# A quantized matrix turned by VectorE in 32x32 blocks, with the block exchange in its store

## The reference

```
xn  = layernorm(x)
s   = causal_attention(xn)            # 32 query heads of 16, one shared key and value head, projected by wo
h   = linear8bit(xn, W1, b1)          # 512 -> 2048
g   = silu(linear8bit(h, W2, b2))     # 2048 -> 512
out = x + s * g

linear8bit(a, W, b): columns of a whose largest |value| is over 3 are outliers;
    y = quant_rows(a without outliers) @ quant_rows(W).T + (outliers of a) @ W.T + b
quant_rows(a): scale = max|row| / 127;  round(a / scale) * scale
```

## Time and profile before

| | us |
|---|---|
| median of three timed runs | 802.89 |
| lowest and highest | 801.82, 803.98 |
| span of the profiled execution | 800.2 |
| PE busy in it | 766.0 |
| DVE busy | 639.8 |
| ACT busy | 404.4 |
| POOL busy | 255.5 |
| attention block, some | 96 to 407 |
| W1 products, some | 409 to 603 |

### The profile page before, as it was taken

One profiled execution on the slowest core, in us unless ns is written; L12 is line 12 of the kernel. 1 busy time (PEld: TensorE's weight loads), 2 busy tenths in 40 slices (PEclk: granted clock), 3 DMA queues, 4 the chain that ended last, 5 costly groups with the idle time before them and its releaser, 6 DMA issues. The chain is left out here.

```text
span 800.2 us, 12098 instructions
## 1 busy us (share of the span) xinstructions
PE 766.0 (96%) x4253; PEld 579.9 (72%) x4253; DVE 639.8 (80%) x1099; ACT 404.4 (51%) x686; POOL 255.5 (32%) x335
## 2 busy tenths in 40 slices
PE   5999899999999999999999999999997999999995
PEld 4878565656676676775578888888886888888884
DVE  7988989999999999995537476666658998599957
ACT  4354166767777666777634544544553333132212
POOL 7213135555555555554521110110100000036504
PEclk9999689999999999999999999999999999999998
DMA  7431303333322223334454443222013778436982
GB/s 265 147 106 53 82 15 87 83 81 85 99 81 83 82 82 85 95 110 123 163 198 150 153 158 138 93 73 79 27 48 101 246 223 259 162 106 223 342 276 105
DMA packets 58348, 103.37 MB, mean 129 GB/s; under 512 B 8480, under 2 KB 16688, under 8 KB 56752
## 3 DMA queue, kind: packets, MB, share of 16 engines
q1 hardware_dynamic: 58288, 102.60, 40.2%
HBM read 52.76 MB, written 36.70 MB: 112 GB/s over the span
## 5 line engine op out<-in xcount | busy, mean ns | idle before, releaser
L931 DVE TENSOR_REDUCE rowmax<-ps 128x2 f32<-128x512 f32 (+3 forms) x384 | 210.6, 590 | 20.3 <-PE ps L1008 18.7
L852 ACT ACTIVATE probs<-ps 128x512 f32<-128x512 f32 (+1 forms) x352 | 175.3, 557 | 71.8 <-PE ps L1021 70.1
L1008 PE MATMUL ps<-km,stack 128*128 128x256 f32 (+3 forms) x512 | 150.3, 348 | 2.6 <-PEq L193 1.9
L1021 PE MATMUL ps<-stack,ks 128*128 128x512 f32 (+1 forms) x352 | 132.8, 387 | 2.6 <-ACT probs L852 2.6
L1008 PEld LDWEIGHTS ps<-km,stack 128*128 128x128 f32 (+1 forms) x512 | 95.1, 199 | 43.1 <-DVE rowmax L931 23.9
L834 POOL TENSOR_SCALAR_AFFINE_SELECT probs<-probs 128x512 f32<-128x512 f32 x128 | 81.0, 641 | 78.0 <-ACT probs L852 76.6
L1823 PE MATMUL ps<-big_h 128*128 128x512 f32 x256 | 100.5, 393 | 2.3 <-issue 2.0
L1825 PE MATMUL ps<-big_h,big_l 128*128 128x512 f32 x256 | 100.1, 391 | 0.0
L1824 PE MATMUL ps<-big_l,big_h 128*128 128x512 f32 x256 | 100.1, 391 | 0.0
L1034 PE MATMUL ps<-probs,vones 128*32 128x512 f32 (+3 forms) x1024 | 82.2, 439 | 0.2 <-POOL probs L834 0.2
L1021 PEld LDWEIGHTS ps<-stack,ks 128*128 128x128 f32 x352 | 67.4, 192 | 11.6 <-ACT probs L852 6.3
(11 more groups left out here) (227 smaller groups left out, 1388.8 us busy)
## 6 DMA issues: line engine op xcount, KB each, us to landing
stack<-big_h SPq DMA_DIRECT2D x128, 64.0 KB, 2.0
h_scratch<-hs SPq DMA_DIRECT2D x7, 1024.0 KB, 4.5
hload<-h_scratch SPq DMA_DIRECT2D x14, 512.0 KB, 5.0
xn_scratch<-xa SPq DMA_DIRECT2D x4, 1024.0 KB, 4.4
stack<-big_l SPq DMA_DIRECT2D x64, 64.0 KB, 2.0
xi<-xn_scratch SPq DMA_DIRECT2D x16, 256.0 KB, 2.7
xe_scratch<-xm SPq DMA_DIRECT2D x16, 256.0 KB, 2.3
w2n<-in_L_ffn_W_dram SPq DMA_DIRECT2D x4, 1024.0 KB, 6.4
```

Source lines behind the costliest of these rows:

```text
L852: nc.scalar.activation(probs[p][:, o:o + nh * w], ps[:, STB[n % NST], 0:nh * w], ACT.Exp).then_inc(s_exp, 1)
L931: nc.vector.tensor_reduce(dst, src, AX_X, ALU.max).then_inc(s_red, 1)
L1008: last = nc.tensor.matmul(dst, stack[u % 3][rows, hp, P * qt:P * (qt + 1)], km[rows, u // KT, p0:p0 + npar, keys], start=True, stop=True)
L1021: ins = nc.tensor.matmul(ps[:, STB[n % NST], 0:nh * w].rearrange("p (h q) -> p h q", h=nh), ks[:, u // KT, p, P * kt:P * (kt + 1)], stack[ ...
```

## The change

DVE transposes in place of PE. Its transpose turns each 32x32 block of a 128x512 tile on its own and leaves the blocks where they are. For a whole 128x128 transpose the blocks must change places too, row block a with column block b within each group of 128 columns. That exchange is put into the store of the quantized tile: four DMAs (`HB`), one for each 32 rows of the tile, write each run of 32 floats to its exchanged place in `xe_scratch`. Loads of that scratch stay as they were; all counts of `s_xes` become four times as large. In the tail, one transpose by DVE stands at the step where PE had four, ahead of the low part of the tile before. In the FFN block `turn_x` of tiles 12 to 15 stands on DVE between `scale_w1(1)` and the low parts; PE's four groups go, ACT's `high_x` waits for `s_tt`, and the counts of `s_aux` are four lower.

```
@@ second block: setup @@
+        HB, SQ = 4, 32
@@ second block: SP @@
                     if u >= 0:
                         sp.wait_ge(s_xe, u + 1)
-                        sp.dma_start(xe_d[P * u:P * (u + 1), :], xm[:, :]).then_inc(s_xes, 16)
+                        for b in range(HB):
+                            sp.dma_start(xe_d[P * u:P * (u + 1), :]
+                                         .rearrange("(a j) (k b i) -> b j k a i", a=HB, k=KT, b=HB)[b],
+                                         xm[SQ * b:SQ * (b + 1), :].rearrange("j (k a i) -> j k a i", k=KT, a=HB)
+                                         ).then_inc(s_xes, 16)
                     i = tail_tile(g, -5)
                     if i >= 0:
-                        sp.wait_ge(s_xes, 16 * (i + 1))
+                        sp.wait_ge(s_xes, 16 * HB * (i + 1))
...
@@ second block: POOL @@
                         if u:
-                            pool.wait_ge(s_xes, 16 * u)
+                            pool.wait_ge(s_xes, 16 * HB * u)
@@ second block: DVE, after quantize_x, ahead of tail_tile(g, 2) @@
+                    i = tail_tile(g)
+                    if i >= 0:
+                        dve.wait_ge(s_tr[i % 2], 16 * (i // 2 + 1))
+                        if i < NMAX:
+                            dve.wait_ge(s_red, CH * U)
+                        else:
+                            dve.wait_ge(s_xlo, i - NMAX + 1)
+                        nc.vector.transpose(ps[:, MAXB[i % NMAX], :], tail_rows[:, i % 2, :]).then_inc(s_tt, 1)
@@ second block: PE @@
-                    i = tail_tile(g)
-                    if i >= 0:
-                        pe.wait_ge(s_tr[i % 2], 16 * (i // 2 + 1))
-                        if i < NMAX:
-                            pe.wait_ge(s_red, CH * U)
-                        else:
-                            pe.wait_ge(s_xlo, i - NMAX + 1)
-                        for k in range(KT):
-                            last = nc.tensor.transpose(ps[:, MAXB[i % NMAX], P * k:P * (k + 1)],
-                                                       tail_rows[:, i % 2, P * k:P * (k + 1)], ident[:, :])
-                        last.then_inc(s_tt, 1)
@@ third block: ACT @@
                 def high_w1(f):
                     n = aux_at[("w1", f)]
-                    act.wait_ge(s_aux, n + 1)
+                    act.wait_ge(s_aux, n + 1 - (NT - EARLY))
...
                 def high_x(i):
                     n = aux_at[("x", i)]
-                    act.wait_ge(s_aux, n + 1)
+                    act.wait_ge(s_tt, i + 1)
...
@@ third block: DVE @@
+                def turn_x(i):
+                    n = aux_at[("x", i)]
+                    dve.wait_ge(s_xel[i - EARLY], 16)
+                    nc.vector.transpose(ps[:, 4 + n % 4, :], xe[i - EARLY]).then_inc(s_tt, 1)
...
                 scale_w1(1)
                 for f in range(FT):
                     if f == 0:
+                        for i in range(EARLY, NT):
+                            turn_x(i)
                         for i in range(EARLY, NT):
                             low_x(i)
                         low_w1(1)
@@ third block: PE @@
-                def transpose_x(i):
-                    dst = aux_bank(("x", i))
-                    pe.wait_ge(s_xel[i - EARLY], 16)
-                    for k in range(KT):
-                        last = nc.tensor.transpose(dst[:, P * k:P * (k + 1)], xe[i - EARLY][:, P * k:P * (k + 1)],
-                                                   ident[:, :])
-                    last.then_inc(s_aux, 1)
...
                     for c in range(NC):
-                        for i in late_x(f, c):
-                            transpose_x(i)
                         if w2_group(f, c) >= 0:
```

More of the change, by code:

```diff
@@ L769, in _ @@
                         sp.wait_ge(s_xm, NT)
-                        sp.wait_ge(s_xes, 16 * (EARLY + 1))
+                        sp.wait_ge(s_xes, 16 * HB * (EARLY + 1))
                         sp.dma_start(inlier_row[:, :], xe_d[P * EARLY:P * (EARLY + 1), :]).then_inc(s_xel[0], 16)
@@ L788, in _ @@
                                      ).then_inc(s_obt if n in TAIL_OUT else s_obs[n % 2], 16)
-                sp.wait_ge(s_xes, 16 * NT)
+                sp.wait_ge(s_xes, 16 * HB * NT)
             @block.gpsimd
@@ L1514, in scale_w1 @@
                     if f > 2:
-                        dve.wait_ge(s_aux, aux_at[("w1", f - 2)] + 1)
+                        dve.wait_ge(s_aux, aux_at[("w1", f - 2)] + 1 - (NT - EARLY))
                     nc.vector.scalar_tensor_tensor(out=w1t[f % 2][:, :], in0=w1n[f % 2][:, :], scalar=cst[:, 1:2],
```

## The result

The changed kernel took **804.41 us** (median of 15 runs, 799.51 to 806.42), the kernel before 801.70 beside it (15 runs, 799.01 to 803.98): a ratio of **1.0032, 95% interval 1.0019 to 1.0044**. It is slower by some 2.7 us. The forecast was 804.7, made from the earlier median of 802.89; as a difference it was +1.8, so part of the agreement comes from the base.

What follows compares the result with a forecast made beforehand. PE was taken as the bound, with DVE close beside it in the middle of attention. The terms summed as 802.89 - 2.3 (tail) + 1.6 (FFN start) + 2.5 (store) = 804.7 us, range 798.5 to 832.

Steps and rivals of the forecast that it cites:

- What bounds the kernel: Whole kernel: PE busy 766.0 and DVE 639.8 of 800.2 us, the two close together mid-attention.
- Parts 1 and 2: PE loses 5.3 us of transposes in the tail, 1.8 in the FFN; DVE gains 8.4 in the tail, at 704 ns each.
- Part 5: Attention stage: four small-run DMAs per store land 5.0 us after the first issue, delaying POOL's mask product; +2.5 us.
- the price of the packet: Store in the attention stage: engine time per 128 B packet written to DRAM, taken as 27.4 ns from 512 B runs.
- my lower value of 16: Store: 16 ns per small packet, estimated from 64 B packets into SBUF; the four issues then set the landing.
- the floor by issues: Store: landing set by the four issues, 3 x 0.58 + 2.0 = 3.8 us, if packets cost 16 ns.
- the units with a low limit by their place: Attention units that bear store landings of only 4.8 us (three) or 4.1 to 4.3 (two), losing 0.2 and 0.8.
- the first rival: Attention stage: dear small writes make the store a loop link above a 4.9 us landing; 816 to 849 us; chance 0.35.
- Part 3: Tail of the attention stage: the last tile's load, transpose and ACT copy come earlier; -2.3 us, ceiling 6.9.
- both come about 1.3 us earlier: Tail: tile 14's store and the last tile's load move 1.3 us earlier, from three PE transpose groups of 0.44.
- Part 4: FFN start: DVE's four transposes delay tile 12's low part, so PE waits some 3 us; +1.6 us.
- The second rival: Attention stage and tail: transfers stay hidden at 16 ns a packet, tail gives 4 to 5 us; 799.5 us; chance 0.15.

Runs made afterwards that it cites:

- e8: Changed kernel with tile 14's store placed behind the load of tile 11 on SP, not ahead of it; 800.33 us, ratio 0.9992 to the kernel before.
- e13: Changed kernel with e6's order on DVE, e8's late store, e11's earlier W1 load and four tail load buffers, not two; 797.47 us, 0.9959 of before.
- e3: Kernel before with exchanging store and DVE transposes for tiles 0 to 11 only, 12 to 15 the old way; 799.80 us, 0.9997 of before.
- e12: Changed kernel with the old single plain store, DVE transposes kept, blocks not exchanged; 802.18 us, ratio 1.0018 to the kernel before.
- e4: Kernel before with exchanging store and DVE transposes for tiles 12 to 15 only, 0 to 11 the old way; 802.37 us, 1.0021 of before.
- e7: Changed kernel with 24 unused PE transposes where PE waits ahead of the W1 transposes; 801.95 us, ratio 1.0005 to the kernel before.
- e6: Changed kernel with DVE's FFN order changed: two transposes, W1 scaling, then low parts and transposes in turn; 802.58 us, 1.0003 of before.
- e11: Changed kernel with e6's order on DVE, e8's late store and W1's load ahead of tile 13's; 800.40 us, ratio 0.9990 to the kernel before.
- e10: Kernel before with each store cut into four plain DMAs of 32 whole rows; 801.99 us, ratio 1.0009 to the kernel before.
- e5: Changed kernel with all four FFN-start transposes ahead of the scaling of W1 tile 1 on DVE; 804.60 us, ratio 1.0054 to the kernel before.

## Why the prediction was right, term by term

- **What bounds the kernel.** Right: PE and DVE run together in the steady stage, and nothing moved there (PE's waits for DVE, 18.3 us in 37, in both).
- **Parts 1 and 2.** Right. DVE's transposes of tail rows take 726 ns (median of 12) and those of the FFN 682 to 719, against the 704 taken from the copy out of PSUM. By these medians, writing to PSUM adds 22 ns at most.
- **Part 5, the store: +2.5, measured +0.95 (S); 0.0 to +1.2 over all kernels with this store.** The step that failed is the price of the packet, 27.4 ns, taken from writes of 512 B. It is 13.1, below even my lower value of 16, and the small runs don't fill the engines. The landing came after 4.35 us, not 5.0: the floor by issues (3.8) was the better model, with a pitch of 0.66 and not 0.58. Who pays was half right: of the three units with a late landing two are those that the prediction named as late already, but they lost 0.05 and 0.16 us and not about 1 each. The largest loss, 0.55, is in a unit that no row of before marks out; the units with a low limit by their place lost next to nothing. The loop of the first rival and its kind of threshold were right; with 11.6 + 1.3 in place of 12.1 + 1.37 it decides from a landing of about 5.4 us. The Trainium skill ("DMA: Bandwidth & Descriptors", Specifications) says that a transfer below 512 B does a read-modify-write and misses the line rate. The second half agrees: 128 B in 13.1 ns against 512 B in 27.4 is half the bytes in the same engine time. But a packet is not dearer, and no run shows whether a read-modify-write takes place.
- **Part 3, the tail: -2.3, measured -0.34.** Two steps failed. The first is "both come about 1.3 us earlier". The last store left at 383.51, 0.09 earlier than before once the shift of 0.95 is taken off. I had moved it by PE's saved time, but SP reaches it through the chain of load and transpose in two buffers, and that doesn't get shorter when PE has less work: it waits on landings. e8 and e13 show that chain by making it shorter: their last transposes come 1.1 and 3.4 us earlier after the start of T. The second is a missing term, the clock: ACT and then PE wait for the new transposes in turn, and PE's clock falls for 3.4 us in six of the seven kernels that have DVE's transposes in the tail, two buffers and the old order on SP (not in e3), and in none of the four with PE's transposes. Between e12 and e3 this is 1.24 us; in after the product at 384.67 took 1.4 more. Where the clock holds, in e3, T is 1.19 shorter than before, half of what was forecast.
- **Part 4, the FFN: +1.6, measured +2.24.** The mechanism was right in its place, order and releaser: PE's first use of tile 12's bank follows an idle time for DVE's low part, 2.26 us against "some 3". By itself this cost 0.65, less than forecast, because W1's load landed 3.2 us after the first FFN product, not 3.8, and DVE's transposes stood 0.6 apart. The landing differs by execution: e4, e7, e8 and e12, with the same order on DVE, turn W1 0.8 to 1.0 us later than before. A slip beside it: PE came to that point 1.6 us earlier, since four groups of transposes went; the prediction put this at 1.3, the length of three. What failed is a missing term: after that wait PE ran at the lower clock for some 3.4 us, 1.6 us lost. e7 took the clock's fall away, e6 all but 0.75 us of the wait as well.
- **The sum.** +1.8 forecast, +2.7 measured: that it is close is luck, because two terms that were too large, of opposite sign, nearly cancelled (+2.5 and -2.3 against +0.95 and -0.34), and the fall of the clock, in no term, made up the rest. The second rival's store was nearest to the truth and its tail farthest.

**Open.** Why single issues or landings are late by about 1 us: in two units they are so in nearly every kernel (272.36 took 3.77 us for four, 1.1 more than the others), elsewhere only now and then. Why the clock fell after a wait of 2.3 us in the kernel after and not after 2.5 in e12, and in the tail of e12 and not of e3. How the 2.7 us of the timed runs divide between the order on DVE and the two falls of the clock is known from single profiled executions only.

## What to carry to other kernels

Work that is moved off a full engine gains only what the chain behind it lets through: look first at who waits on landings (here two load buffers), and shorten that, as four buffers did. On the engine that receives the work, write out the order in which its inputs arrive and in which its results are needed; here the wrong order made the FFN's start 3 us longer than the right one (F 15.69 and 12.62). An earlier load doesn't help if another load that the same queue needs first moves behind it (e11). And count a wait on TensorE as more than its length: it may be followed by some microseconds at half the clock, and a stretch of one execution should be compared with another only after a look at the granted clock in both.

## What the runs showed of the hardware

- Writes of 128 B runs to DRAM cost 13.1 ns of one DMA engine each, half of a 512 B packet's 27.4. Four DMAs of 512 such runs were issued 0.66 us apart, four of 32 rows of 2 KB 0.50 apart, at an engine share of only 0.63.
- Splitting a store of 256 KB into four, without small runs, moved its landing from at most 2.4 to 3.4 us after the first issue (e10).
- After 2.26 us without work PE ran at full clock for 1.4 us, then for 3.4 us at the lower level. 24 transposes in the wait kept it at 1.00. One execution with such a wait (e12, 2.51 us) did not fall.
- In the tail PE's clock fell for 3.4 us behind waits of 0.8 to 1.4 us in after, e5, e6, e7, e11 and e12, and held in e3 behind one of 1.11 and in before behind one of 0.84. At the lower level 32 value products took 3.98 us up to the next product, at the upper 2.74.
